# Rows of score maxima turned in 32x32 blocks on VectorE instead of by TensorE, and moved by four transfers instead of one

## What is computed

```python
x_norm = modulate(_ln(x), shift_a, scale_a)
q, k, v = split(x_norm @ W_qkv + b_qkv)                  # 16 heads of 16
attn_w = softmax(einsum('bhqd,bhkd->bhqk', q, k) * scale)
x = x + gate_a[:, None] * (attn_out @ W_proj + b_proj)
q_c = _ln(x) @ W_qc + b_qc;  k_c, v_c = split(_ln(context) @ W_kvc + b_kvc)
c_attn_w = softmax(einsum('bhqd,bhsd->bhqs', q_c, k_c) * scale)
x = x + c_attn_out @ W_cproj + b_cproj
h = gelu(modulate(_ln(x), shift_m, scale_m) @ W_mlp1 + b_mlp1)
return x + gate_m[:, None] * (h @ W_mlp2 + b_mlp2)
```

## Time and profile before

| | us |
|---|---|
| median of 3 runs | 980.63 |
| lowest and highest run | 976.08, 981.22 |
| span of the profiled execution | 980.9 |

### The profile page before, as it was taken

The page is one execution under the profiler, slowest core; times in us unless marked ns, Lnnn a source line. Parts: engine busy times, 40 slices in busy tenths (PEclk is TensorE's granted clock), DMA queues, the critical chain, the costliest instruction groups (busy, mean ns, idle before and its releaser), DMA issues.

```text
span 980.9 us, 19308 instructions
## 1 busy us (share of the span) xinstructions
PE 897.5 (91%) x7216; PEld 657.4 (67%) x7216; DVE 617.9 (63%) x1302; ACT 590.5 (60%) x1058; POOL 348.2 (35%) x398
## 2 busy tenths in 40 slices
PE   5487899999999999999999999999999999997967
PEld 4355566677776767676777767677777767665736
DVE  3437678767767776767767767577677776644220
ACT  2142556849585767667594948567684958482522
POOL 4604044326161615253342616153433524120212
PEclk9668789999999999999999979899999999798779
DMA  7774635363445363534436333735436361130001
GB/s 214 150 101 73 105 68 107 74 86 78 91 85 86 71 116 66 107 79 82 83 82 93 80 74 74 112 67 91 92 75 88 70 90 43 34 55 33 23 0 33
DMA packets 77311, 79.21 MB, mean 81 GB/s; under 512 B 9729, under 2 KB 71810, under 8 KB 76834
## 3 DMA queue, kind: packets, MB, share of 16 engines
q1 hardware_dynamic: 76930, 77.43, 42.3%
q10 hardware_dynamic: 288, 0.54, 0.1%
HBM read 22.82 MB, written 4.26 MB: 28 GB/s over the span
## 4 chain that ended last, share of the span: by engine, by line
PE 76%; DVE 6%; ACT 4%; DMA 4%; SPq 4%; issue 4%; POOL 2%; POOLq 0%; ACTq 0%; DVEq 0%
PE bank L544 18%; PE scan L640 14%; PE pv L596 12%; PE bank L583 11%; PE bank L554 6%; PE bank L574 5%; PE score L650 4%; PE bank L525 3%; SPq L322 3%; DVE MX_y L927 2%; PE bank L563 2%; DMA QS_y<-SQ_y 2%; ACT P L781 2%; DVE MX_x L927 1%; DMA QS_x<-SQ_x 1%
## 5 line engine op out<-in xcount | busy, mean ns | idle before, releaser
L781 ACT ACTIVATE P<-score 128x512 f32<-128x512 f32 x512 | 289.0, 595 | 202.2 <-PE score L650 197.9
L927 DVE TENSOR_REDUCE MX_y<-scan 128x2 fp32r<-128x512 f32 x256 | 168.3, 681 | 83.2 <-PE scan L640 82.8
L927 DVE TENSOR_REDUCE MX_x<-scan 128x2 fp32r<-128x512 f32 x256 | 170.8, 679 | 78.0 <-PE scan L640 78.0
L640 PE MATMUL scan<-KS_x,QS_x 48*128 48x256 f32 x512 | 121.4, 336 | 25.8 <-DVE MX_x L927 16.2
L467 POOL TENSOR_TENSOR y<-y,x_bias 128x256 f32<-128x256 f32 x32 | 23.3, 728 | 329.7 <-DVE y L895 329.7
L544 PE MATMUL bank<-xT_y,W 128*128 128x256 f32 x960 | 136.1, 292 | 2.3 <-DVE xT_y L835 1.7
L544 PEld LDWEIGHTS bank<-xT_y,W 128*128 128x128 f32 x960 | 121.8, 194 | 14.2 <-DVE xT_y L835 6.9
L583 PE MATMUL bank<-w_down,HH 128*128 128x256 f32 x512 | 129.5, 399 | 1.0 <-ACT HH L734 1.0
L640 PE MATMUL scan<-KS_y,QS_y 48*128 48x256 f32 x512 | 111.3, 327 | 19.8 <-DMA QS_y<-SQ_y 8.0
L650 PE MATMUL score<-QS_y,KS_y 49*128 49x256 f32 x512 | 116.8, 330 | 8.1 <-ACT P L781 6.3
L640 PEld LDWEIGHTS scan<-KS_x,QS_x 48*128 48x128 f32 x512 | 76.6, 196 | 68.9 <-issue 30.3
(11 more groups left out here) (109 smaller groups left out, 1316.7 us busy)
## 6 DMA issues: line engine op xcount, KB each, us to landing
KS_x<-SK SPq DMA_DIRECT2D x96, 128.0 KB, 4.3
QS_x<-SQ_x SPq DMA_DIRECT2D x96, 128.0 KB, 4.5
KS_y<-SK SPq DMA_DIRECT2D x96, 128.0 KB, 4.4
QS_y<-SQ_y SPq DMA_DIRECT2D x192, 64.0 KB, 2.6
x_in<-in_x SPq DMA_DIRECT2D x16, 256.0 KB, 2.7
c_in<-in_ctx SPq DMA_DIRECT2D x16, 256.0 KB, 2.9
gate_a<-d_gate SPq DMA_DIRECT2D x16, 256.0 KB, 3.4
gate_m<-d_gate SPq DMA_DIRECT2D x16, 256.0 KB, 3.5
```

Of the source, the lines that this page charges most:

```text
L640: scanned = nc.tensor.matmul(scan_bank[n % NSCAN][:, i * N:(i + 1) * N], QS[s1][b1 % 2][row:row + 3 * HD, p, i * 128:(i + 1) * 128], KS[s1 ...
L781: nc.scalar.activation(P[:, s % 8, :, :].rearrange("p a n -> p (a n)"), score_bank[s % 2][:, :], ACT.Exp, scale=SCALE).then_inc(s_exp, 1)
L927: nc.vector.tensor_reduce(MX[s1][:, half, :, par, p], scan_bank[n % NSCAN][:, :].rearrange("p (a n) -> p a n", a=NB), AXIS.X, ALU.max, neg ...
```

## The change

TensorE and ScalarE have no part in the maxima any more. `MX` becomes 128 partitions by two halves by 32 columns, of which 16 are used: column 2 * (head index in the half) + query half. VectorE turns each half with one `STREAM_TRANSPOSE`, which turns each 32x32 block (32 partitions by 32 columns) on its own, into `MT`, one tile for each attention. So the result lies in four groups of 32 partitions, and in each group 16 partitions hold 32 queries of all 8 heads. SyncE moves each group by a transfer of its own, 16 partitions by 128 bytes, 2 KB: four in place of one. The wait before the scores becomes 64 in place of 16. Two VectorE instructions at the start clear `MX`.

`SP_PLAN` is not changed. `PE_PLAN` and `ACT_PLAN` lose their four `max` entries. `DVE_PLAN` gets `max_x0` in section A at slot 7, `max_x1` in A at slot 15, `max_y0` in B at slot 7 and `max_y1` in B at slot 15, each right behind the last maximum of its half. The four tasks leave `BANKED`.

```diff
-          ("T_y", -1, 8), ("max_x0", 0, 9), ("pv_y1", -2, 9), ("q_ya", -1, 9), ("q_yb", -1, 9), ("q_xa", 1, 12),
+          ("T_y", -1, 8), ("pv_y1", -2, 9), ("q_ya", -1, 9), ("q_yb", -1, 9), ("q_xa", 1, 12),
...
-          ("stats_y", -1, 5), ("norm_y", -1, 7), ("k_x", 1, 7), ("T_y", -1, 8), ("pt_y0", -2, 8), ("q_y", -1, 10),
-          ("pn_y0", -2, 15), ("q_x", 1, 15), ("po_y0", -2, 15)],
+          ("stats_y", -1, 5), ("norm_y", -1, 7), ("max_x0", 0, 7), ("k_x", 1, 7), ("T_y", -1, 8), ("pt_y0", -2, 8), ("q_y", -1, 10),
+          ("max_x1", 0, 15), ("pn_y0", -2, 15), ("q_x", 1, 15), ("po_y0", -2, 15)],
...
             def maxima(s, half, b):
                 sp.wait_ge(s_MT[s][half], b + 1)
-                sp.dma_start(QS[s][b % 2][3 * HD:3 * HD + 65:64, 4 * half:4 * half + 4, :].bitcast(fp32),
-                             MT[half][:, :].bitcast(fp32)).then_inc(s_row[s][half], 16)
+                rows = QS[s][b % 2][3 * HD:3 * HD + 65:64, 4 * half:4 * half + 4, :].bitcast(fp32)\
+                    .rearrange("r p (a i n) -> r (p a) i n", a=NB, i=4)
+                for i in range(4):
+                    sp.dma_start(rows[:, :, i, :], MT[s][32 * i:32 * i + 2 * PAIRS, half, :]).then_inc(s_row[s][half], 16)
...
-            def maxima(s, half, b):
-                pe.wait_ge(s_scan_done, SCANS[s, b] + PAIRS * (half + 1))
-                to = take(f"max_{s}{half}", b)
-                for a in range(NB):
-                    last = nc.tensor.transpose(to[0:PAIRS, a * 128:(a + 1) * 128],
-                                               MX[s][:, half, a, :, :].rearrange("p b c -> p (b c)").bitcast(fp32),
-                                               ident[:, :])
-                last.then_inc(s_full, 1)
...
-                        pe.wait_ge(s_row[s2][s // PAIRS], 16 * (b2 + 1))
+                        pe.wait_ge(s_row[s2][s // PAIRS], 4 * 16 * (b2 + 1))
...
-            def maxima(s, half, b):
-                if s == "x":
-                    wait(act, s_row["y"][half], 16 * (b - 1))
-                else:
-                    act.wait_ge(s_row["x"][half], 16 * min(b + 2, B))
-                src = full(act, f"max_{s}{half}", b)
-                nc.scalar.activation(MT[half][:, :], src[0:PAIRS, 0:N], ACT.Copy).then_inc(s_MT[s][half], 1)
...
+            def maxima(s, half, b):
+                dve.wait_ge(s_scan_done, SCANS[s, b] + PAIRS * (half + 1))
+                wait(dve, s_row[s][half], 4 * 16 * b)
+                nc.vector.transpose(MT[s][:, half, :], MX[s][:, half, :].bitcast(fp32)).then_inc(s_MT[s][half], 1)
```

More of the change, by code:

```diff
@@ L31 @@
 PE_PLAN = {
-    "A": [("up0a", -3, 0), ("up1a", -3, 0), ("up0b", -3, 0), ("up1b", -3, 0), ("pv_x3", -1, 1), ("max_y1", -2, 1),
+    "A": [("up0a", -3, 0), ("up1a", -3, 0), ("up0b", -3, 0), ("up1b", -3, 0), ("pv_x3", -1, 1),
           ("v_xa", 0, 2), ("v_xb", 0, 2), ("T_x", 1, 3), ("up2a", -3, 3), ("up2b", -3, 5), ("out_xa", -1, 5),
           ("out_xb", -1, 5), ("k_xa", 1, 7), ("k_xb", 1, 7), ("up3a", -3, 7), ("up3b", -3, 7), ("pv_y0", -2, 7),
-          ("T_y", -1, 8), ("max_x0", 0, 9), ("pv_y1", -2, 9), ("q_ya", -1, 9), ("q_yb", -1, 9), ("q_xa", 1, 12),
+          ("T_y", -1, 8), ("pv_y1", -2, 9), ("q_ya", -1, 9), ("q_yb", -1, 9), ("q_xa", 1, 12),
           ("q_xb", 1, 13), ("pv_y2", -2, 14)],
-    "B": [("pv_y3", -2, 0), ("max_x1", 0, 0), ("v_ya", -1, 1), ("v_yb", -1, 1), ("down0a", -3, 1), ("down0b", -3, 3),
+    "B": [("pv_y3", -2, 0), ("v_ya", -1, 1), ("v_yb", -1, 1), ("down0a", -3, 1), ("down0b", -3, 3),
           ("T_c", 0, 3), ("out_ya", -2, 5), ("out_yb", -2, 5), ("pv_x0", 0, 5), ("k_ya", 0, 7), ("k_yb", 0, 7),
-          ("max_y0", -1, 8), ("pv_x1", 0, 8), ("T_m", -2, 10), ("down1a", -3, 12), ("down1b", -3, 14),
+          ("pv_x1", 0, 8), ("T_m", -2, 10), ("down1a", -3, 12), ("down1b", -3, 14),
           ("pv_x2", 0, 14)],
@@ L42 @@
 ACT_PLAN = {
-    "A": [("up0", -3, 0), ("up1", -3, 0), ("max_y1", -2, 2), ("v_x", 0, 2), ("T_x", 1, 3), ("up2", -3, 5),
-          ("k_x", 1, 6), ("up3", -3, 7), ("T_y", -1, 7), ("q_y", -1, 9), ("max_x0", 0, 9), ("q_x", 1, 13)],
-    "B": [("max_x1", 0, 0), ("v_y", -1, 2), ("T_c", 0, 3), ("k_y", 0, 7), ("max_y0", -1, 8), ("T_m", -2, 12)],
+    "A": [("up0", -3, 0), ("up1", -3, 0), ("v_x", 0, 2), ("T_x", 1, 3), ("up2", -3, 5),
+          ("k_x", 1, 6), ("up3", -3, 7), ("T_y", -1, 7), ("q_y", -1, 9), ("q_x", 1, 13)],
+    "B": [("v_y", -1, 2), ("T_c", 0, 3), ("k_y", 0, 7), ("T_m", -2, 12)],
 }
@@ L59 @@
 }
-BANKED = {"up0", "up1", "up2", "up3", "max_x0", "max_x1", "max_y0", "max_y1", "out_x", "out_y", "T_c", "T_y", "T_x",
+BANKED = {"up0", "up1", "up2", "up3", "out_x", "out_y", "T_c", "T_y", "T_x",
           "T_m", "k_x", "q_x", "k_y", "q_y", "v_x", "v_y", "down0", "down1"}
-HALVED = BANKED - {"T_c", "T_y", "T_x", "T_m", "max_x0", "max_x1", "max_y0", "max_y1"}
+HALVED = BANKED - {"T_c", "T_y", "T_x", "T_m"}
 def within(b):
@@ L160, in build @@
         rsum = sb("rsum", [128, 2, 8])
-        MX = {s: sb(f"MX_{s}", [128, 2, NB, 2, PAIRS // 2], f32r) for s in "xy"}
-        MT = [sb(f"MT{i}", [PAIRS, N], f32r) for i in range(2)]
+        MX = {s: sb(f"MX_{s}", [128, 2, 32], f32r) for s in "xy"}
+        MT = {s: sb(f"MT_{s}", [128, 2, 32]) for s in "xy"}
         stats = {k: sb(f"stats_{k}", [128, NB, 6]) for k in "xycm"}
@@ L262, in emptied @@
                 return s_HH, FB // 2 * b + int(s) + 1
-            if kind == "ma":
-                return s_MT[name[4]][int(name[5])], b + 1
             if kind == "do":
@@ L603, in _ @@
                 **{f"pv_{s}{g}": lambda b, s=s, g=g: weighted(s, g, b) for s in "xy" for g in range(4)},
-                **{f"max_{s}{h}": lambda b, s=s, h=h: maxima(s, h, b) for s in "xy" for h in range(2)},
                 **{f"T_{k}": lambda b, k=k: transposes(f"T_{k}", k, b) for k in "xycm"},
@@ L899, in _ @@
                    (("pt", turned), ("pn", normed), ("po", returned)) for s in "xy" for h in range(2)},
+                **{f"max_{s}{h}": lambda b, s=s, h=h: maxima(s, h, b) for s in "xy" for h in range(2)},
                 "out_x": out_x,
@@ L926, in slot @@
                     dve.wait_ge(s_scan_full, n + 1)
-                    nc.vector.tensor_reduce(MX[s1][:, half, :, par, p],
+                    col = NB * (PAIRS // 2 * par + p)
+                    nc.vector.tensor_reduce(MX[s1][:, half, col:col + NB],
                                             scan_bank[n % NSCAN][:, :].rearrange("p (a n) -> p a n", a=NB),
@@ L958, in gates @@
                 nc.vector.tensor_tensor(rows[:, 3, :], rows[:, 3, :], rows[:, 2, :], ALU.mult).then_inc(s_rowsC, 1)
+            for k in "xy":
+                nc.vector.memset(MX[k][:, :, :].bitcast(fp32), 0.0)
             dve.wait_ge(s_exp0, 1)
```

1 line of the change is left out of this document (removed), and 4 rows, old and new, of the table DVE_PLAN.

## The result

The changed kernel is slower: a median of 1011.47 us (1006.61 to 1014.5, 4 runs) against 980.92 us (976.08 to 984.04, 4 runs) of the kernel before, a ratio of 1.033 with an interval of 1.029 to 1.038. The forecast was 998 us, with a range of 975 to 1024. The profiled execution has a span of 1004.8 us.

The account below looks back on a forecast made before the run. TensorE, busy 91%, was taken as the bound, except ahead of section B, where ScalarE, SyncE and transfers decide. 980.9 - 20 + 24 + 1 = 986 us, plus 12 for the clock, gave 998 us; range 975 to 1024 us.

Parts of the forecast that it names:

- TensorE's saving: 64 turns of the maxima leave TensorE, 0.31 us each, with no pause before or behind: -20 us.
- The later start of B: Three more issues of max_x0 behind q_y0 on SyncE, up to 1.8 us a step before section B: +24 us.
- the 15 terms: Delays at the 15 starts of B: 1.8 us in ten, then 1.4, 1.3, 1.3, 1.8 and 0.6 us.
- VectorE: 64 turns added on VectorE, estimated 0.19 us each, which might hold up scans: +1 us, bounds 0 and +12.
- The other three rows: Added issues for max_x1, max_y0 and max_y1 on SyncE, hidden by TensorE's work in the slots between: cost nothing.
- the copies on ScalarE: 64 copies of 361 ns leave ScalarE, which isn't the bound: 0 taken, with a bound of -5 us.
- The clock: Longer TensorE idle time before B brings 1.2 GHz behind about 9 of 14 starts: +12 us, bounds 0 and +37.
- credit of 13 us: Taken off the 25 us clock cost for five steps of the kernel before that already hold low-clock stretches.
- The first (the transfers are hidden, 961 us): Rival: the small transfers before B cost nothing, so only TensorE's 20 us saving stays; chance 0.13.
- The second (a later start, the clock as before, 986 us): Rival: B starts later as worked out, but the clock does as before, 982 to 990 us; chance 0.23.
- The third: Rival: low clock behind every start of B, and VectorE's turns delay scans, about 1029 us; chance 0.14 with the fourth.
- The fourth: Rival: small transfers take much longer to land than the 8 KB one, time as the third; chance 0.14 with it.

Follow-up runs that it names:

- e3: Changed kernel with each row of maxima filled by one 8 KB transfer of zeros, VectorE's turns kept, maxima not taken off; 962.95 us, ratio 0.983.
- e10: Changed kernel with eight extra identity matmuls on TensorE ahead of the wait at slot 0 of section B; 982.06 us, ratio 1.004.
- e2: Kernel before, turns on TensorE kept, with all four rows of maxima moved by four 2 KB transfers each; 1023.42 us, ratio 1.045.
- e5: Kernel before with only the row of max_x0 moved by four 2 KB transfers, the other three rows by one each; 1024.84 us, ratio 1.050.
- e6: e1 with every VectorE turn of the maxima done twice, the extra one into a scratch tile; 962.13 us, ratio 0.985.
- e1: Changed kernel with max_x0 moved ahead of q_y0 in SyncE's table, all small transfers kept; 964.26 us, ratio 0.985 to the kernel before.
- e4: Changed kernel with twelve extra identity matmuls on TensorE ahead of the wait at slot 0 of section B; 988.56 us, ratio 1.009.
- e8: Kernel before with four extra identity matmuls on TensorE ahead of the wait at slot 0 of section B; 985.23 us, ratio 1.008.
- e7: e1 with two of the six transfers of q_y0 issued by ScalarE right behind SQ_y, instead of by SyncE; 995.8 us, ratio 1.021.

## Why the prediction was right, and the term that was not

The direction, the place and the mechanism were right, and the time was inside the range, 13 us above the forecast. To add up the parts I take differences of the ratios, since the experiments ran on several chips, times 981 us: -16 (e3), +20 (e3 to e10) and +29 (e10 to the changed kernel) make the 33 us that the whole change costs by its ratio; by the two medians it is 30.5 us.

These three parts still mix the clock with the rest, and the clock can be taken out. With two levels, a run's time at the low level is twice (1 - mean granted clock) times its span. On average that is 119 us in the kernel before (49 runs), 117 us in e3, 102 us in e10 and 177 us in the changed kernel; most of it lies at the start and the end of the program in all of them. From e10 to the changed kernel 29 us of time go with 74 us more at the low level, 0.39 us for each; between the runs of the kernel before it is 0.33 us. With that the parts become, as estimates, about -16 us for the turns, +26 us for the later start and +23 us for the clock.

**TensorE's saving, predicted -20 us, measured -16 us (e3), and as much without the clock.** The turns themselves are gone as worked out, 1.25 us a step. What eats into it are the two new waits shown above: in e3 they are 6.3 us longer in total than before, while e2 and e5, which keep TensorE's turns, have them in 3 and 2 places as the kernel before. The turn of `max_x0` had stood between `T_y` and `q_ya`, and TensorE's 0.31 us there covered VectorE's `xT_y`; without it the projection waits in 15 steps (4.8 us in total in the changed kernel, 1.7 before), and the turn of the MLP's `xn_y` now comes too early for GpSimd in 15 steps instead of 3 (8.8 us against 6.3). The prediction called TensorE's work "without a pause before and behind it" for all 64 turns; it doesn't hold behind these. The row I read the earlier trace rows shows what follows a turn; I had not asked what the turn hid.

**The later start of B, predicted +24 us, measured +20 us (e10 against e3), about +26 us without the clock.** The size of the shift is right, 1.57 us a step where 1.6 us was the mean of the 15 terms. The issue is a little cheaper than assumed, 0.50 to 0.52 us in most cases against 0.55 to 0.60.

**VectorE, predicted +1 us and 0.19 us a turn, measured 0 and 0.21 us (e6).** The estimate from the forms of the earlier trace rows was good.

**The other three rows, and the copies on ScalarE, predicted 0.** The first is shown by e2 against e5. The second is not told apart by any run.

**The clock, predicted +12 us net, measured about +23 us net.** This is the term that was mis-sized. It was a gross cost of 25 us less a credit of 13 us. The gross cost was nearly right, 29 us (e10 against the changed kernel), by two errors that cancel. The count was too low: I took 9 of 14 starts, from four rows of which one was at 1.00; it set in at or behind 13 of 14, and at the last it was there already. The price of each was too high: 29 us over 14 is 2.0 us, against 2.8 us assumed. The credit was about twice too large. It stood for the five low-clock steps that the kernel before already had; but the kernel before spends only 17 us more at the low level than e10, which is worth about 6 us. And it was taken as if these steps would be among the dipped ones anyway, while three of the five fell elsewhere, late in section A.

**The rivals.** The first (the transfers are hidden, 961 us) is refuted by the 40.1 us of wait, and yet its time is what the change gives in another place of the queue, 964 us. The second (a later start, the clock as before, 986 us) is nearly e10: 982 us, and about 988 us with the low-level time of the kernel before added. It was right about the later start and wrong about the clock. The third had nearly the right count, every start, but too high a price for each (3.6 us, where 2.0 us was measured), and 6 us for VectorE where nothing showed. The fourth is refuted: the fourth small transfer lets B start 1.78 us behind its issue, the 8 KB one did 1.94 us.

**What was to show it.** B 1.9 us behind the fourth issue and 3.7 behind the first (1.8 and 3.5); idle time near 2 us (2.15 to 3.11, somewhat longer); TensorE's busy time at full clock 1.2 us less, 50.2 us (in e1, which has steps at full clock, 50.0 us against 51.4 us); a full-clock step 0.4 us longer: no step is at full clock, and those nearest to it (0.97) are 2.1 us longer than 52.55. Of these 2.1 us, -1.25 are the turns, +0.4 the two new waits, +1.57 the later start and about +1.35 the clock.

## What to carry to other kernels

A transfer's price is also its place in the queue that issues it: ask what stands in front of the issue that a waiting engine needs last, and put behind it whatever was ready earlier. Here four issues for one cost 5% (from e3 to the changed kernel) behind the six of another operand and nothing at all ahead of them, where their data had long been ready. When an instruction is taken out of the busiest engine, look at what it hid on the others before counting its time as saved, and where idle time grows on TensorE, price the clock behind it as a term of its own, and take a credit for low-clock stretches that are there already only where the trace shows that the same wait brings them.

## What the runs showed of the hardware

- The granted clock and TensorE's idle time before a start of B, from 146 to 884 us: the changed kernel and e2 have 28 starts with 1.88 us or more of idle time. At 25 of them the low level sets in behind the wait or during it, at two (859.22 and, in e2, 883.73) it had begun over 2 us ahead of the wait, and at one (1.90 us, e2) it does not come. In e5 it is 11 of 12 between 200 and 823 us; the one without it has 1.89 us. In e1 and e3 most starts have 0.5 to 1.7 us, and two in each run are followed by it; the longest, 1.93 us in e1, isn't. Filling the idle time with matmuls on the identity took the low level away from 173 to 835 us (e4, e10) and made the kernel 29 us faster (e10). That the idle time is what matters and not the start of B itself is shown by this; that no other thing matters isn't, see e8.
- Behind a wait of only 0.55 us, late in section A, the clock fell to 1.2 GHz, three times in e8 and three times in the kernel before, while TensorE was busy (6.60 of 6.60 us in e8, 3.42 of 3.42 us in the kernel before). I had not expected that, and most waits of this length are not followed by it.
- A transfer of 2 KB and one of 8 KB between two SBUF tiles take about the same time from issue to the start of the engine that waits, 1.78 us against 1.94 us. The issue costs SyncE's queue nearly the same for any size here, in the median 0.50 to 0.52 us for 2 KB, 0.55 us for 8 KB, 0.59 us for 64 KB and 0.60 us for 128 KB, and 0.6 us of ScalarE's instruction stream (1.21 us for two).
- In e7 SyncE issued its four transfers of `q_y0` and ScalarE its two side by side (351.91 and 351.92). In these cases the time from SyncE's first issue of `q_y0` to its last is 2.19 us, against 3.19 us in e1 (at 449.34), so the queue time saved was real, and it was the issuing engine that paid.
